# Delta stage of a four-stage kernel: q, k, v and beta projections from pairs of fp16 numbers instead of fp32

## The reference

```python
h = _rms(x, attn_norm_w)                              # x: layer-normed rows
q = silu(silu(_causal_dwconv(h @ Wq.T, conv_q)))      # 4 taps over the 32 rows of a sequence
k = silu(silu(_causal_dwconv(h @ Wk.T, conv_k)))
v = silu(silu(_causal_dwconv(h @ Wv.T, conv_v)))
q, k = _l2norm(q), _l2norm(k)                         # per head, 32 heads of 16 features
beta = jax.nn.sigmoid(h @ Wbeta.T)                    # one number for a row and a head
o = _delta_scan(k, q, v, beta)                        # 32 steps, state of 16 by 16 for each head
x = x + _rms(o, out_norm_w) @ Wout.T
```

## Time and profile before

| | |
|---|---|
| median of 3 runs | 3780.47 us (3779.79 to 3780.53) |
| the profiled execution | 3776.57 us |
| its span, first to last instruction | 3774.2 us |
| busy: PE, PEld, DVE, ACT, POOL | 81%, 46%, 58%, 35%, 13% of the span |
| mean granted TensorE clock | 0.90 of full speed |

### The profile page before, as it was taken

How to read it: one execution, slowest core, us unless ns; L and a number is a source line. 1 busy time by engine, 2 the same in 40 slices (tenths; PEclk the granted TensorE clock), 3 DMA queues, 4 the chain that set the end, 5 groups by cost and what they waited for, 6 DMA issues and landing times. The chain is left out here.

```text
span 3774.2 us, 69666 instructions
## 1 busy us (share of the span) xinstructions
PE 3074.3 (81%) x27622; PEld 1728.9 (46%) x27622; DVE 2205.9 (58%) x3340; ACT 1309.6 (35%) x2002; POOL 481.0 (13%) x206
## 2 busy tenths in 40 slices
PE   6888888886858877788787479999999539999998
PEld 3444444442434444544445234444444226666665
DVE  4333333433799898898898633333333377666665
ACT  2221222213435344343443132222222115656565
POOL 0000000001000000000000000000000017767766
PEclk9999999997868889789887589999999769999999
DMA  5344444302000100101000041111111310111110
GB/s 189 120 134 134 134 134 134 111 24 77 18 1 2 35 11 26 36 2 35 25 13 25 24 154 45 56 56 56 56 56 45 132 56 31 42 36 39 36 39 31
DMA packets 112459, 227.02 MB, mean 60 GB/s; under 512 B 10784, under 2 KB 15776, under 8 KB 110848
## 3 DMA queue, kind: packets, MB, share of 16 engines
q1 hardware_dynamic: 112256, 224.09, 17.4%
HBM read 182.11 MB, written 41.94 MB: 59 GB/s over the span
## 5 line engine op out<-in xcount | busy, mean ns | idle before, releaser
L1841 POOL TENSOR_TENSOR d_zb<-d_za 128x1024 f32<-128x1024 f32 x32 | 75.4, 2356 | 2395.5 <-DVE d_za L1914 2395.5
L815 PE MATMUL b_e<-b_hT,b_wqkv 128*128 128x512 f32 x768 | 331.7, 593 | 0.0
L1198 DVE TENSOR_TENSOR b_tmp<-b_L,b_U 128x1984 f32<-128x1984 f32 (+30 forms) x248 | 301.4, 1215 | 14.9 <-ACT b_L L976 10.7
L1200 DVE TENSOR_TENSOR b_U<-b_U,b_tmp 128x1984 f32<-128x1984 f32 (+30 forms) x248 | 303.7, 1225 | 8.5
L1526 DVE SCALAR_TENSOR_TENSOR c_av<-c_r,c_sg 128x512 f32<-128x512 f32 x88 | 60.8, 691 | 417.2 <-PE c_r L1398 409.6
L1398 PE MATMUL c_r<-c_hT,c_g_pair 128*128 128x512 f16 x1056 | 262.4, 402 | 12.7 <-DVE c_hT L1517 12.7
L1398 PE MATMUL c_r<-c_hT,c_u_pair 128*128 128x512 f16 x1056 | 243.7, 380 | 0.0
L1398 PE MATMUL c_d<-c_d_pair,c_aT 128*128 128x512 f16 x1056 | 241.0, 379 | 0.0
L1706 PE MATMUL d_m<-d_wb,d_xiT 128*128 128x512 bf16 x1024 | 229.1, 382 | 3.7 <-ACT d_xiT L1820 2.4
L815 PEld LDWEIGHTS b_e<-b_hT,b_wqkv 128*128 128x128 f32 x768 | 145.3, 190 | 186.6 <-issue 186.6
L1145 DVE SCALAR_TENSOR_TENSOR b_raw<-b_e,b_cw,b_raw 128x496 f32<-128x496 f32 (+2 forms) x288 | 201.3, 715 | 39.5 <-ACT b_raw L990 30.1
(11 more groups left out here) (234 smaller groups left out, 5424.1 us busy)
## 6 DMA issues: line engine op xcount, KB each, us to landing
a_cn<-in_ctx SPq DMA_DIRECT2D x128, 512.0 KB, 5.4
a_x_ln<-in_x SPq DMA_DIRECT2D x8, 1024.0 KB, 6.3
a_cw<-in_ctx SPq DMA_DIRECT2D x128, 64.0 KB, 5.7
a_x_res<-in_x SPq DMA_DIRECT2D x32, 256.0 KB, 3.4
x<-a_x_out SPq DMA_DIRECT2D x32, 256.0 KB, 2.0
b_xg<-x SPq DMA_DIRECT2D x8, 1024.0 KB, 5.6
b_xr<-x SPq DMA_DIRECT2D x32, 256.0 KB, 2.7
xm<-b_xr SPq DMA_DIRECT2D x32, 256.0 KB, 2.1
```

The lines of the kernel that those rows point to most:

```text
L815: mm = pe.matmul(p[:], w_qkv[:, i, k, c * P:(c + 1) * P], hT[:, k, :], start=(k == 0), stop=(k == DC - 1))
L1198: V.tensor_tensor(tmp[:, :, s + 1:S, :], lo, us, ALU.mult).then_inc(prod, 1)
L1200: V.tensor_tensor(U[:, :, s + 1:S, :], U[:, :, s + 1:S, :], tmp[:, :, s + 1:S, :], ALU.subtract).then_inc(sub, 1)
L1841: nc.gpsimd.tensor_tensor(o[:, :, 0, :], a[:, :, 0, :], a[:, :, 1, :], ALU.add).then_inc(bf, 1)
```

## The change

The delta stage's q, k, v and beta products are formed from pairs of fp16 numbers in three matmuls each. `w_qkv` and `w_b` become fp16 with an axis of two (hi, lo), in the same bytes; `hT` is read as fp16 pairs `hp`, in the same bytes too. The fp32 weights are loaded into `raw` and `Up` first (the same 13 loads, the same bytes), ScalarE makes the hi parts, VectorE the lo parts. GpSimd scales the norm weights (`hvec`) and the taps `cw` (by 1/(256*64), which takes the scales out again), and clears `Up` only after the weights are split. ScalarE and VectorE wait for that clearing. For each group ScalarE writes the hi rows from banks h0 to h3, and VectorE the lo rows in a new `low_rows`, called behind `solve` step 0 of the body; VectorE now frees these banks.

```diff
-        w_qkv = sb("wqkv", [P, 3, DC, D])
-        w_b = sb("wb", [P, DC, NH])
+        w_qkv = sb("wqkv", [P, 2, 3, DC, D], F16)
+        w_b = sb("wb", [P, 2, DC, NH], F16)
...
+        hp = hT_all[:].bitcast(F16).rearrange("p (i c n) -> p i c n", i=2, n=GT)
...
+        WS, HS = 256.0, 64.0
+        STAGED = tuple((raw_all[:, i * DC * D:(i + 1) * DC * D], src.rearrange("p c n -> p (c n)"),
+                        w_qkv[:, :, i].rearrange("p j c n -> p j (c n)")) for i, src in enumerate((wq, wk, wv)))
+        STAGED += ((Up[:, 0:DC * NH], wbeta.rearrange("p c n -> p (c n)"), w_b[:].rearrange("p j c n -> p j (c n)")),)
...
@@ gpsimd
+            pool.wait_ge(loaded, 16 * len(LOADS))
+            nc.gpsimd.tensor_scalar(hvec[:], vec[:, 0], HS, None, ALU.mult).then_inc(vec_ready, 1)
+            nc.gpsimd.tensor_scalar(cw[:], cw[:], 1 / (WS * HS), None, ALU.mult).then_inc(vec_ready, 1)
+            pool.wait_ge(w_ready, len(STAGED))
             nc.gpsimd.memset(Up[:], 0.0).then_inc(zeroed, 1)
-            pool.wait_ge(loaded, 16 * len(LOADS))
...
@@ tensor
             pe.wait_ge(wo_ready, DC)
+            pe.wait_ge(w_ready, len(STAGED))
...
@@ betas
-                    mm = pe.matmul(p[2 * NH:3 * NH, :], w_b[:, k, :], hT[:, k, :], start=(k == 0), stop=(k == DC - 1))
+                    for i, j in ((0, 0), (0, 1), (1, 0)):
+                        mm = pe.matmul(p[2 * NH:3 * NH, :], w_b[:, i, k, :], hp[:, j, k, :],
+                                       start=(k + i + j == 0), stop=(k == DC - 1 and i == 1))
...
@@ project
-                        mm = pe.matmul(p[:], w_qkv[:, i, k, c * P:(c + 1) * P], hT[:, k, :],
-                                       start=(k == 0), stop=(k == DC - 1))
+                        for a, b in ((0, 0), (0, 1), (1, 0)):
+                            mm = pe.matmul(p[:], w_qkv[:, a, i, k, c * P:(c + 1) * P], hp[:, b, k, :],
+                                           start=(k + a + b == 0), stop=(k == DC - 1 and a == 1))
...
@@ scalar
+            act.wait_ge(loaded, 16 * len(LOADS))
+            for src, _, pair in STAGED:
+                A.activation(pair[:, 0], src, ACT.Copy, scale=WS).then_inc(w_hi, 1)
             act.wait_ge(zeroed, 1)
-            act.wait_ge(loaded, 16 * len(LOADS))
+            act.wait_ge(vec_ready, 2)
...
-                    p, free = E.take(act, g, f"h{c}")
-                    A.activation(hT[:, c, :], p[:], ACT.Copy, scale=vec[:, 0, c:c + 1]).then_inc(free, 1)
+                    p, _ = E.take(act, g, f"h{c}")
+                    A.activation(hp[:, 0, c, :], p[:], ACT.Copy, scale=hvec[:, c:c + 1]).then_inc(h_hi, 1)
...
@@ vector
-            dve.wait_ge(loaded, 16 * len(LOADS))
+            for i, (src, _, pair) in enumerate(STAGED):
+                dve.wait_ge(w_hi, i + 1)
+                V.scalar_tensor_tensor(pair[:, 1], src, WS, pair[:, 0], ALU.mult, ALU.subtract).then_inc(w_ready, 1)
             dve.wait_ge(zeroed, 1)
+            dve.wait_ge(vec_ready, 2)
+
+            def low_rows(g):
+                for c in range(DC):
+                    p, free = E.take(dve, g, f"h{c}")
+                    dve.wait_ge(h_hi, g * DC + c + 1)
+                    V.scalar_tensor_tensor(hp[:, 1, c, :], p[:], hvec[:, c:c + 1], hp[:, 0, c, :],
+                                           ALU.mult, ALU.subtract).then_inc(free, 1)
...
                     if do["cur"]:
                         solve(k, s)
+                    if do["next"] and s == 0:
+                        low_rows(k + 1)
```

More of the change, by code:

```diff
@@ L664, in delta_phase @@
         vec = sb("vec", [P, 2, DC])
+        hvec = sb("hvec", [P, DC])
         ident = sb("ident", [P, P])
@@ L686, in delta_phase @@
         osq = hT
-        raw = sb("raw", [P, DC, 3, GT])
+        hp = hT_all[:].bitcast(F16).rearrange("p (i c n) -> p i c n", i=2, n=GT)
+        raw_all = sb("raw", [P, DC * 3 * GT])
+        raw = raw_all[:].rearrange("p (c i n) -> p c i n", i=3, n=GT)
         stat = sb("stat", [3 * NH, GT])
@@ L711, in delta_phase @@
         loaded, eps_ready, wo_ready, zeroed = sem("loaded"), sem("eps"), sem("wo"), sem("zeroed")
+        w_hi, w_ready, vec_ready, h_hi = sem("w_hi"), sem("w_ready"), sem("vec_ready"), sem("h_hi")
         x_ready = sem("x_ready")
@@ L726, in delta_phase @@
         block = stack.enter_context(nc.Block())
-        LOADS = ((w_qkv[:, 0], wq), (w_qkv[:, 1], wk), (w_qkv[:, 2], wv), (w_b[:], wbeta), (w_o[:], wout),
-                 (cw[:], conv), (vec[:], vecs), (ident[:], consts["ident"]), (heads[:], consts["heads"]),
+        LOADS = tuple((dst, src) for dst, src, _ in STAGED) + (
+                 (w_o[:], wout), (cw[:], conv), (vec[:], vecs), (ident[:], consts["ident"]), (heads[:], consts["heads"]),
                  (spread[:], consts["spread"]), (own[:], consts["own"]), (past[:], consts["past"]),
@@ L979, in rows @@
                 for c in range(DC):
-                    p, free = E.take(act, g, f"h{c}")
-                    A.activation(hT[:, c, :], p[:], ACT.Copy, scale=vec[:, 0, c:c + 1]).then_inc(free, 1)
+                    p, _ = E.take(act, g, f"h{c}")
+                    A.activation(hp[:, 0, c, :], p[:], ACT.Copy, scale=hvec[:, c:c + 1]).then_inc(h_hi, 1)
             def betas(r):
                 p, free = R.take(act, r, "beta")
-                A.activation(stat[2 * NH:3 * NH, :], p[2 * NH:3 * NH, :], ACT.Tanh, scale=0.5).then_inc(free, 1)
+                A.activation(stat[2 * NH:3 * NH, :], p[2 * NH:3 * NH, :], ACT.Tanh, scale=0.5 / (WS * HS)).then_inc(free, 1)
             def taps(g, c):
```

## The result

The changed kernel takes **3799.5 us** (median of 5 runs, 3798.5 to 3801.5) against 3780.5 for the kernel before on the same chip (3779.8 to 3782.4): a ratio of 1.005, with a 95% interval of 1.0035 to 1.0064. The prediction was 3804. The profiled execution took 3798.7 us with a span of 3796.2, 22.0 us more than the span before. The question for the runs is where these 22 us sit, and why the 65 us that TensorE's busy time fell by gave nothing back.

The account below looks back on a forecast made before the run. VectorE was taken to bound the groups beside a solve. Start +2.2 and seven groups +21.0 give +23.2 on the profiled 3776.6, so 3799.8; with the median 3.9 above, 3803.7, say 3804 us, range 3794 to 3822.

Parts of the forecast that it names:

- VectorE sets the pace, TensorE's gain beside a solve is nothing: Seven groups beside a solve: VectorE's 10.5 us a chunk covers TensorE's new 7.8, so cheaper projections gain nothing.
- `low_rows` 18.9 us: Seven groups: four added VectorE instructions between solve steps cost 2.7 us a group, never given back later.
- the rival by which they absorb the work: VectorE's 4.5 us a group of waiting for `out` swallows the added 2.7; total 3783 us, chance 0.07.
- The restart, 0.3 a group: Seven groups: TensorE stands 6.6 us, resumes at low clock, and VectorE waits for q0; 2.1 us in all.
- the rival: Seven groups: low clock lasts through q0, so VectorE waits 3.5 us a group; 3826 us, chance 0.18.
- The bounds of 0 and 3.5 a group: VectorE's wait at a group's first banks: nothing if q0 is in time, 3.5 us if low clock lasts through q0.
- The start, +2.2: Stage's start and first group: 12.6 us later plus 0.8 for `low_rows`, less 0.9 in `betas` and 10.3 in projections.
- A gain of 0.9: First group's `betas`: 5.9 us before, about 5.0 as twelve fp16 matmuls at 1.2 GHz.
- The signs: Expected in the trace: group period longer by 2.7 to 3 us, first transposes 12 to 13 later, v3 about 2 later.
- TensorE as the bound (3704): Convolutions wait for banks, so faster projections count in all eight groups: 90 us saved, 13.4 spent; chance 0.04.
- The slow restart (3826): Seven groups: TensorE's low clock lasts through q0, VectorE waits 3.5 us in each; chance 0.18.
- The rate of the Trainium skill's page: First group: fp16 matmuls at 131 ns, 1.57 us a bank, 4.6 us less in all; 3799 us, chance 0.03.

Follow-up runs that it names:

- experiment 1: Changed kernel without `low_rows`; matmuls that would read the lo rows read the hi rows again: 3777.8 us, ratio 0.999 to the kernel before.
- experiment 5: Changed kernel with only the hi-by-hi product, one in place of three, for q, k, v and beta: 3786.2 us, ratio 1.0015.
- experiment 6: Changed kernel with a fourth product, lo by lo, in the projections, sixteen matmuls a bank: 3831.2 us, ratio 1.0138.
- experiment 2: Changed kernel with `low_rows` ahead of solve step 0 in place of behind it: 3794.3 us, ratio 1.003.
- experiment 3: Changed kernel with 28 matmuls of overwritten result added in every group to fill TensorE's stand: 3799.7 us, ratio 1.0049.
- experiment 4: Changed kernel with 28 matmuls of overwritten result added only in the seven groups beside a solve: 3798.0 us, ratio 1.0045.
- experiment 7: Changed kernel with `Up` cleared under the loads, first rows' statistics before the weights' splitting, and TensorE's weight waits moved later: 3790.3 us, ratio 1.0022.
- experiment 10: Changed kernel with the lo rows made by GpSimd from a second, fp32 copy of the rows, not by VectorE: 3829.5 us, ratio 1.0132.
- experiment 9: Changed kernel with both `low_rows` ahead of solve step 0 and the reordered start: 3784.7 us, ratio 1.0008.
- experiment 8: Kernel before, fp32 projections kept, with first rows' statistics ahead of the weights' wait and TensorE's `w_o` wait in `out`: 3775.7 us, ratio 0.9983.

## Why the prediction was right, step by step

**VectorE sets the pace, TensorE's gain beside a solve is nothing: shown.** The kernel without `low_rows` has TensorE's saving and the groups of before (experiment 1), and one product in place of three gives no more than the restart's waits (experiment 5). It holds for the kernel before. Beside the new `low_rows` a slower pace would have cost (experiment 6), which the prediction did not need to say.

**`low_rows` 18.9 us: shown, with 19.6.** 2.64 instead of 2.7 a group, plus a delay of 0.23 that I had not counted in most of them. None of it was given back later: the waits for `out` are as long as before, so the rival by which they absorb the work fell.

**The restart, 0.3 a group: the mis-sized term.** Measured 5.9 us over the seven groups, 0.8 each, where the sum has 2.1. The length of the stand was right (6.84 us for 6.6), and q0 came almost as worked out: it cost 1.3 us in seven groups, and in four of them nothing. The low clock lasted 5.1 us in the mean where I had taken 4.5. What was missing is the rest, 4.6 us: with q0 just in time, k and v come 2.59 us apart and VectorE needs one in 2.22, so that each waits 0.37. I had worked that out only for the rival and left it out of the main case, where it holds as well. The bounds of 0 and 3.5 a group held it. Experiments 2, 3 and 4 take the wait away, by an earlier restart or by a full clock. (The rows' windows of 0.79 and 0.86 put the clock's two earlier returns at 1440.4 and 894.3, 4.6 and 9.1 us after work resumed, not 4.4 and 8.9; the sum hardly moves by it.)

**The start, +2.2: the second mis-sized term.** Measured +0.1. The statistics came 12.6 us later, the first group's projections gained 41.4 - 31.25 = 10.2, both as worked out. The error sits in `betas`: I had them at the low clock with 5.0 us, as the earlier trace rows show, but the clock had risen before they began, and they took 2.76. A gain of 0.9 was one of 3.2. The 1-us window ahead of them:

```profile
902.00:903.00 1.00, 0.07 (x1) 0.00 (x0) 0.85 (x2) 0.69 (x1) 0.00 (x0) 0.93 0.00 0
```

The two errors partly cancel, 3.8 us too little in the groups and 2.1 too much at the start, and the stage's end came 0.7 us sooner: +24.2 us for the stage was measured and +23.2 predicted. That the sum is so near is in part luck. The profiled execution came out 1.1 us below the 3799.8 of the sum: +1.0 in the stage, +0.8 ahead of it, -3.0 in the later stages, which hold nothing of the change. The other 3.1 us by which the median lies under 3804 are the distance of median and profiled execution, 3.9 for the kernel before and 0.8 for this one.

**The signs.** The four `low_rows` instructions, the later transposes and the smaller share of TensorE came as named. Three signs did not: a group's period grew by 3.5 us in the mean (24.8 over seven) and not by 2.7 to 3; there was idle time of 0.37 before k and v, and not only before a group's first bank; and v3 of the first group ended 0.7 us later, not 2. They are the two mis-sized terms again.

**The rivals.** TensorE as the bound (3704) fell with experiments 1 and 5. The slow restart (3826) happened by a quarter of its price. The rate of the Trainium skill's page (TensorE: Matmul & The Clock Gate, Back-to-back issue gap, 131 ns) does not hold here: 144 matmuls in 31.25 us are 217 ns each.

**What it comes to.** The change trades some 11 us a group of an engine that isn't the bound for 2.7 of one that is. It pays only in the first group, and there the splitting of the weights and its place ahead of the statistics take the gain away. The start can be mended (experiment 7), the restart too (experiment 2); the 2.7 a group can't be moved to GpSimd (experiment 10), and what is left comes out level with before (experiment 9), 9.0 us behind the kernel before with the same better start (experiment 8).

## What to carry to other kernels

Before making an engine's work cheaper, cut the stage into windows and see which engine is full there; the page's share of the whole span named TensorE, and the windows named VectorE. Price the helper work that a cheaper form needs (here the low halves, and what a queue of preparations holds up behind it) on the engine that does it, and ask what stands idle while it runs: TensorE came back from 6.8 us of standing at half its clock, which cost a third as much again as the added instructions. When an engine is found to be just in time for a first item, compare its pace with its consumer's for the next ones too. And an idle engine is no free place for added work if the two slow each other down (experiment 10).

## What the runs showed of the hardware

TensorE's return to 2.4 GHz came 3.9 to 5.7 us after work resumed, behind stands of 6.8 us in seven groups; when useless matmuls filled all but 0.69 us of the stand, the twelve next matmuls took 2.76 us in place of 5.30. At the changed kernel's start sixteen short transposes, spread over 3.65 us, were followed by a granted clock of 0.93 although TensorE then stood for 1.6 us; in the kernel before the same sixteen began at 885.20, and the clock rose only at 894.3.

GpSimd and VectorE beside each other cost more than I had expected. In experiment 7 the four scalings of `w_o` ran beside VectorE's splitting of the weights and took 11.4 us, where they took 6.19 in the changed kernel, while VectorE's three pieces took 7.11 in place of 6.69:

```profile
878.36 11.41 POOL L790 TENSOR_SCALAR b_wo<-b_wo,b_vec 128x512 f32<-128x512 f32 x4
```

A total can hide what a trace shows: stretches of the program that no edit touched differed by up to 4.4 us between the profiled executions of two kernels, as much as some of the effects looked for, so an effect below some 5 us was read from marks in the trace and not from medians.
